# Writing ALiBi's distances with ScalarE into the scores' banks, the first projections by halves, and a new order of engine work

## The reference

```python
def _L0_attn_ref(hidden_states, Wq, bq, Wk, bk, Wv, bv, Wo, bo, alibi_slopes):
    ...
    scores = jnp.einsum('bhsd,bhtd->bhst', q, k)
    rel = (pos[None, :] - pos[:, None]).astype(scores.dtype)
    bias = alibi_slopes[:, None, None] * rel
    scores = (scores + bias[None]) / math.sqrt(HD)
    scores = 30.0 * jnp.tanh(scores / 30.0)
    scores = jnp.where(causal[None, None], scores, -jnp.inf)
    probs = jax.nn.softmax(scores, axis=-1)
    ...
x = x + _L0_attn_ref(_layernorm(x), ...)        # self attention, causal, ALiBi
x = x + _L0_xattn_ref(_layernorm(x), ctx_2048, mask_BxS2_bk0)   # one head, 128 memory tokens
x = x + _L0_ffn_ref(_layernorm(x), ...)         # silu(gate) * up, then down; weights rounded to fp8 e4m3
```

## Time and profile before

| | us |
|---|---|
| median of 3 runs (557.02 to 558.56) | 558.46 |
| the profiled execution | 558.21 |
| its span, first to last instruction | 556.4 |
| PE busy | 543.5 (98%) |
| DVE, POOL, ACT busy | 361.7, 287.1, 268.5 |
| DMA over the span | 50.74 MB, 91 GB/s |

### The profile page before, as it was taken

How to read it: one execution, slowest core, us unless ns; L and a number is a source line. 1 busy time by engine, 2 the same in 40 slices (tenths; PEclk the granted TensorE clock), 3 DMA queues, 4 the chain that set the end, 5 groups by cost and what they waited for, 6 DMA issues and landing times.

```text
span 556.4 us, 10168 instructions
## 1 busy us (share of the span) xinstructions
PE 543.5 (98%) x3962; PEld 427.4 (77%) x3962; DVE 361.7 (65%) x699; ACT 268.5 (48%) x485; POOL 287.1 (52%) x260
## 2 busy tenths in 40 slices
PE   7999999999999999999899999999999999999997
PEld 7788888888878888888687888766686667866675
DVE  7998877899596796659777886355623564244422
ACT  6848976777765785765743441033401333023310
POOL 5298898965774568787774346134400333013320
PEclk9999999999999999999899999999999999999999
DMA  8951231463217110148832712100011000100001
GB/s 306 347 199 39 78 99 54 124 194 103 77 39 223 43 58 21 58 153 258 275 150 77 264 26 89 57 1 0 1 38 39 0 1 0 58 19 1 0 20 57
DMA packets 43422, 50.74 MB, mean 91 GB/s; under 512 B 2544, under 2 KB 25072, under 8 KB 43376
## 3 DMA queue, kind: packets, MB, share of 16 engines
q1 hardware_dynamic: 43088, 49.58, 26.8%
q10 hardware_dynamic: 288, 0.52, 0.3%
HBM read 36.46 MB, written 13.63 MB: 90 GB/s over the span
## 4 chain that ended last, share of the span: by engine, by line
PE 83%; POOL 8%; DVE 4%; issue 2%; ACT 2%; DMA 1%; DVEq 0%; ACTq 0%; POOLq 0%
PE bank L287 34%; PE bank L452 23%; PE bank L472 16%; PE bank L282 2%; PE bank L394 2%; PE bank L379 2%; PE bank L404 2%; POOL q_w L740 2%; POOL q_w L738 2%; POOL probs L731 1%; POOL x_res L754 1%; PE bank L334 1%; DVE q_m L1228 1%; PE bank L371 1%; POOL reduced L723 1%
## 5 line engine op out<-in xcount | busy, mean ns | idle before, releaser
L287 PE MATMUL bank<-reduced 128*128 128x512 f32 x936 | 224.4, 396 | 1.5 <-ACT probs L897 1.1
L287 PEld LDWEIGHTS bank<-reduced 128*128 128x128 f32 x936 | 173.8, 189 | 39.8 <-issue 1.5
L837 POOL TENSOR_TENSOR f_parts<-fused,f_parts 128x512 fp32r<-128x512 f32 x48 | 62.5, 1301 | 159.9 <-ACT f_parts L1075 159.9
L1057 ACT ACTIVATE tanh_g<-bank,half_gate 128x512 f32<-128x512 f32 x48 | 33.0, 688 | 149.2 <-PE bank L452 139.0
L472 PE MATMUL bank<-reduced,f_parts 128*128 128x512 f32 x384 | 88.4, 390 | 0.0
L472 PEld LDWEIGHTS bank<-reduced,f_parts 128*128 128x128 f32 x384 | 71.9, 188 | 15.0
L1395 DVE SCALAR_TENSOR_TENSOR silu<-tanh_g,bank 128x512 f32<-128x512 f32 x48 | 32.9, 685 | 62.7 <-ACT tanh_g L1057 62.6
L452 PE MATMUL bank<-reduced 128*128 128x512 f32 x288 | 72.0, 402 | 0.0
L452 PEld LDWEIGHTS bank<-reduced 128*128 128x128 f32 x288 | 54.1, 188 | 12.9
L738 POOL TENSOR_TENSOR q_w<-q_w,q_m 128x512 f32<-128x512 f32 x36 | 49.6, 1379 | 9.2 <-DVE q_m L1230 9.2
L731 POOL TENSOR_SCALAR_AFFINE_SELECT probs<-probs 128x1024 f32<-128x1024 f32 x32 | 36.2, 1136 | 34.6 <-ACT probs L904 34.6
(11 more groups left out here) (119 smaller groups left out, 737.1 us busy)
## 6 DMA issues: line engine op xcount, KB each, us to landing
quantized<-q_w SPq DMA_DIRECT2D x36, 256.0 KB, 3.3
reduced<-quantized SPq DMA_DIRECT2D x12, 512.0 KB, 6.8
memT_sb<-in_memT SPq DMA_DIRECT2D x16, 256.0 KB, 5.1
mem_sb<-in_mem SPq DMA_DIRECT2D x16, 256.0 KB, 5.8
out<-y_sb SPq DMA_DIRECT2D x16, 256.0 KB, 2.0
q_w<-in_gate_w SPq DMA_DIRECT2D x12, 256.0 KB, 3.2
q_w<-in_up_w SPq DMA_DIRECT2D x12, 256.0 KB, 3.1
x_res<-in_x SPq DMA_DIRECT2D x3, 1024.0 KB, 9.4
```

Of the source, the lines that this page charges most:

```text
L287: ins = pe.matmul(dst, stationary, moving, start=(n == 0), stop=(n == len(pairs) - 1))
L837: pool.tensor_tensor(f_lo[:, f, :], fused[:, f % 2, :], f_hi[:, f, :].bitcast(F32), ALU.subtract).then_inc(f_lo_ready, 1)
```

## The change

Seven parts. (A) For (g, hg) = (1,1), (1,2), (2,2) and (3,2) the four matmuls of L371 are gone. ACT writes slope times distance into banks 2 to 5 instead, four instructions out of one 128x128 tile `distance`, made by POOL once all of `place_n` has been used. (B) The second halves of the first Q and K go to banks 6 and 7, each half is drained for itself, and the scores' third tile waits for them. (C) All four x tiles are loaded by SP; the high part of the first piece of Wq is made by POOL. (D) `bias_through` is put after the third V projection. (E) On POOL `low_part(g, 0)` stands between the two halves of `causal(g, 2)`, and `norm_scale(1, g-1)` behind both. (F) DVE: `cross(g-2, 6)` before the last slabs of hg 0; `masks` behind `norm_shift`; all four tiles of the second norm behind `x_low`. (G) At the feed forward's start `cross(2, 1)` on ACT and DVE is put ahead of two slabs, `high(0, 1)`, `fuse(0, 1)` and `normalize_context(3, 3)`, with the copy of T2 ahead of the exp; `gate_up` takes each bank only when its first matmul is due.

```diff
+SEEDED = ((1, 1), (1, 2), (2, 2), (3, 2))
...
+                first = [take((name, 0, 0), b) for name, b in (("Q", Q_BANK), ("K", K_BANK))]
+                second = [take((name, 0, 0), b) for name, b in (("Q2", C_BANK), ("K2", E_BANK))]
...
-                    pe.wait_ge(w_hi_made, m + 1)
-                    part(m, first, w_hi, xT_hi, start=True)
-                    if m == 0:
-                        turn_x(0, 3, S_BANK + 3)
+                pe.wait_ge(w_first_made, 1)
+                part(first, 0, w_hi, xT_hi, start=True)
+                turn_x(0, 3, S_BANK + 3)
+                pe.wait_ge(w_hi_made, 1)
+                part(first, 1, w_hi, xT_hi, start=True)
...
+                    if g == 0 and hg == 0 and i == 2:
+                        wait_drained(pe, ("Q2", g, hg))
+                        wait_drained(pe, ("K2", g, hg))
...
+            def scores_onto(g, hg):
+                dst = [take(("S", g, hg, j), S_BANK + j) for j in range(4)]
+                pe.wait_ge(seeded, (SEEDED.index((g, hg)) + 1) * 4)
+                wait_drained(pe, ("Q", g, hg))
+                wait_drained(pe, ("K", g, hg))
+                for i in range(GT):
...
+                        ins = pe.matmul(dst[j][0][:, t], kT[rows, t], qT[rows, t], start=False, stop=(i == GT - 1),
+                                        skip_group_check=True)
...
-                seats = [take((name, g, f), banks[w]) for w, name in ((0, "G"), (1, "U"))]
                 if g == 0:
-                    for w, (dst, done) in enumerate(seats):
+                    for w, name in ((0, "G"), (1, "U")):
+                        dst, done = take((name, g, f), banks[w])
...
-                    if g == 0 and i == 0:
+                    if g == 0 and i == 2:
                         bias_through()
...
-            for i in range(0, GT, 2):
+            for i in range(GT):
                 sp.dma_start(x_res[:, i, :], x_t[:, i, :]).then_inc(x_first_loaded[i], 16)
...
+                if i == 2:
+                    pool.wait_ge(raw_loaded[0], 16)
+                    pool.tensor_copy(w_hi[:, 0, :, FIRST], raw[0].rearrange("p (k n) -> p k n", k=KT)[:, :, FIRST])\
+                        .then_inc(w_first_made, 1)
...
+            pool.wait_ge(bias_made, 2 * HG)
+            pool.iota(distance[:], pattern=[[-1, S]], base=0, channel_multiplier=1,
...
+                slabs = slabs_at(ROUNDED, g, 2)
+                causal(g, 2, (0,))
                 if g:
                     low_part(g, 0)
+                causal(g, 2, (2,))
                 if g:
                     norm_scale(1, g - 1)
...
-                causal(g, 2)
                 low_part(g, 1)
...
+            def seed(g, hg):
+                if (g, hg) == SEEDED[0]:
+                    act.wait_ge(distance_made, 1)
+                for j in range(4):
+                    wait_drained(act, ("S", g, hg - 1, j))
+                    act.activation(bank[S_BANK + j][:].rearrange("p (i s) -> p i s", i=GT),
+                                   distance[:].unsqueeze(1).to_broadcast([P, GT, S]), ACT.Copy,
+                                   scale=slope_all[:, (hg - 1) * 4 + j:(hg - 1) * 4 + j + 1]).then_inc(seeded, 1)
...
-            for i in range(1, GT, 2):
-                act.dma_start(x_res[:, i, :], x_t[:, i, :]).then_inc(x_first_loaded[i], 16)
...
-            weight_high(0)
...
-            q_out(0, 0)
-            k_out(0, 0)
+            for items in (("Q", "K"), ("Q2", "K2")):
...
                     q_out(g, 1)
                     k_out(g, 1)
+                if g == 1:
+                    seed(g, 1)
...
                 q_out(g, 2)
                 k_out(g, 2)
+                if g:
+                    seed(g, 2)
...
             gate(0, 1)
+            cross(G - 2, 1)
             flag_slabs(slabs_at(FLAGGED, G - 1, 3))
             high(0, 1)
-            cross_first(G - 2, 1)
...
                     cross(g - 2, 5)
+                    cross(g - 2, 6)
                     prepare_slabs(slabs[2:])
-                    cross(g - 2, 6)
-                    masks(g - 1)
...
                     norm_shift(g + 1)
+                    if g >= 2:
+                        masks(g - 1)
...
-                if g:
-                    norm_apply(1, g - 1, g - 1, range(1))
...
-                    norm_apply(1, g - 1, g - 1, range(1, GT))
+                    norm_apply(1, g - 1, g - 1)
...
             fuse(0, 0)
+            cross(G - 2, 1)
             fuse(0, 1)
             normalize_context(G - 1, 3)
-            cross(G - 2, 1)
```

More of the change, by code:

```diff
@@ L327, in first_qk, with part @@
             def first_qk():
-                banks = [take((name, 0, 0), (Q_BANK, K_BANK)[m]) for m, name in enumerate("QK")]
-                def part(m, cols, w, t, start=False, stop=False):
-                    dst, done = banks[m]
+                first = [take((name, 0, 0), b) for name, b in (("Q", Q_BANK), ("K", K_BANK))]
+                second = [take((name, 0, 0), b) for name, b in (("Q2", C_BANK), ("K2", E_BANK))]
+                def part(half, m, w, t, start=False, stop=False):
+                    (dst, done), cols = half[m], slice(0, 2 * S) if half is first else slice(2 * S, TG)
                     for k in range(KT):
@@ L335, in part @@
                                         stop=stop and k == KT - 1)
-                    return ins, done
-                first, second = slice(0, 2 * S), slice(2 * S, TG)
+                    if stop:
+                        ins.then_inc(done, 1)
                 pe.wait_ge(xT_hi_ready, 2)
-                for m in range(2):
-                    pe.wait_ge(w_hi_made, m + 1)
-                    part(m, first, w_hi, xT_hi, start=True)
-                    if m == 0:
-                        turn_x(0, 3, S_BANK + 3)
+                pe.wait_ge(w_first_made, 1)
[3 more added lines that the diff above has]
+                part(first, 1, w_hi, xT_hi, start=True)
                 for i in range(2):
@@ L359, in first_qk @@
                 for m in range(2):
-                    ins, done = part(m, second, w_hi, xT_lo, stop=True)
-                    ins.then_inc(done, 1)
+                    part(second, m, w_hi, xT_lo, stop=True)
             def scores(g, hg):
@@ L445, in gate_up @@
                     return
+                seats = []
                 for n, high in enumerate((f % 2 == 0, f % 2 == 1)):
-                    for w, (dst, done) in enumerate(seats):
+                    for w, name in ((0, "G"), (1, "U")):
+                        if n == 0:
+                            seats.append(take((name, g, f), banks[w]))
+                        dst, done = seats[w]
                         for k in range(KT):
@@ L978, in _ @@
             act.wait_ge(small_loaded, 16)
-            q_out(0, 0)
-            k_out(0, 0)
+            for items in (("Q", "K"), ("Q2", "K2")):
+                for name, dst, bias in zip(items, (qT, kT), (bq_c, bk_c)):
+                    src, cols = wait_filled(act, (name, 0, 0)), slice(0, 2 * S) if name in "QK" else slice(2 * S, TG)
+                    act.activation(dst[:, cols], src[:, cols], ACT.Identity, bias=bias[:, 0:1])\
+                        .then_inc(drain_sem((name, 0, 0)), 1)
             weight_high(V_PART)
```

75 lines of the change are left out of this document (49 added, 26 removed).

## The result

The changed kernel takes 552.02 us (median of 6 runs, 551.94 to 552.46), the kernel before, run beside it, 557.75 (6 runs, 556.68 to 559.91). The ratio is 0.9888, 95% interval 0.9872 to 0.9904. The prediction was 551.4, in a range of 549.0 to 555.2. The profiled execution took 551.98, with a span of 550.0 against 556.4: 6.4 us less, where the sum had 7.03.

A forecast was written before the change was run, and what follows sets the result against it. PE, busy 98% of the span, was taken as the bound, with POOL second from 60 to 115 us. Terms of 0.77, 0.30, 0.75, 1.13, 0.34 and 3.74 made 7.03: 558.21 to 551.2, or 551.4 against the median; range 549.0 to 555.2.

The forecast's parts named there:

- Start (halves): At the first scores, K's products start at 16.64 rather than 17.41, as the first halves are long drained: 0.77 us gained.
- Start (x0 alone): At the kernel's start, the first x tile, issued first by SP, lands earlier: 0.3 us, between minus 0.2 and 0.87.
- x1 later than DVE wants it: Lower bound for loading x by SP alone: the second x tile comes too late for DVE, minus 0.2 us.
- POOL's order: At context(1,2), masks end at about 113.4 and bank 6 is late next: context starts 0.75 us earlier.
- POOL keeps the early gains: Rival, 60 to 115 us: slab loads set POOL's queue, so 1.07 and 0.75 are lost: 553.2 us; chance 0.13.
- Readout: At Q's projection, 156.44 us: DVE drains the last readout ahead of the slab, removing PE's whole 1.13 us wait.
- Seeds: Four score groups without bias matmuls: 0.34 us each for (2,2) and (3,2), nothing counted for (1,1) and (1,2).
- The ACT price: Four ACT writes into PSUM per seeded score group: 1.3 to 5.4 us, taken as 2.7.
- Feed forward's entry with seed (3,2): Exp placed first; gate_up(0,3) starts at 270.4 instead of 272.93 and runs at full clock: 3.74 us, 0.34 from the seed.
- The clock's 1.21: At gate_up(0,3), 28 products take 6.63 rather than 7.84 us because the clock does not fall: 1.21 us.
- The later feed forward "does not change": After the feed forward's entry: no wait there and no change, so nothing counted.
- the prediction's case of one more POOL instruction to wait out: At the feed forward's entry, norm tile 0 waits out another 1.3 us POOL instruction: gain there 2.4, time 552.5 us.

The follow-up runs named there:

- two queues again: The changed kernel with x's tiles 1 and 3 loaded by ACT again, tiles 0 and 2 by SP: 551.73 us, ratio 0.9879.
- the three other orders: The changed kernel with norm_scale and norm tile earlier near 303 us, low_part(1, 0) before both masks, gate_up(0,3)'s banks reversed: 551.49 us; repeated, 551.75 with seeds, 551.76 without.

## Why the prediction was right

The forecast was 0.6 us low, and its mechanism stands: five gains at five places, none taken back by a long wait. That the total came so close is in part luck. A lead counted 0.47 too high and a seed 0.2 too high stand against an entry 0.4 too low, and a gain of 0.6 that was not foreseen against a loss of 1.0. By its steps:

- **Start (halves): 0.77 predicted, 0.77 measured.** The copies took 0.47 where 0.48 was taken. Undone alone it costs 0.78 at the scores and 0.4 at the end.
- **Start (x0 alone): 0.30, measured 0.20, by luck.** The tile came 0.47 earlier as the argument has it, but then the third tile was late. The bound "x1 later than DVE wants it" was the right worry, about the wrong tile. The start moved from 0.17 later to 0.62 earlier than before over eleven traces, and with two queues again it was 0.29 earlier, so the 0.20 isn't shown to be the loads' doing.
- **POOL's order: 0.75 on top of a kept lead, to 1.82 at context(1,2); measured 1.35.** The next wait is the one named, bank 6 by DVE's L1236. Undoing the order costs 0.8 at the end, and the wait there grows by 0.94. What was too high is the lead brought there: bank 6 came free only 0.55 earlier (113.49 against 114.04), where the start's whole 1.07 was counted. Part of the start's gain is lost already at a mask (a wait of 0.32 us, at 54.6). That is what the rival "POOL keeps the early gains" had in mind, at a quarter of its size (0.47 of 1.82).
- **Readout: 1.13, measured 1.19,** and 1.2 of span when undone. That the row's releaser, tanh, was wrong is shown: with the old order in the new kernel, the profile itself names DVE.
- **Seeds: 0.34 each for two, measured 0.18 to 0.22.** This term was sized nearly twice too high. From the start of the four bias matmuls to PE's next work was 1.33 us at (1,2) (105.80 to 107.13); from the start of L406 it is 1.11 (104.86 to 105.97). The bias matmuls had covered the first weight loads of the scores (PEld's L379 began at 105.91, 0.23 ahead of its matmul), which now stand bare; that is the reading of these rows. The ACT price was right: 0.68 an instruction, 2.52 for four. At the end of the changed kernel no run shows a gain from seeds, as the two traces differ in the store; with the three other orders a gain of 0.6 is there at the end.
- **Feed forward's entry with seed (3,2): 3.74, measured 4.1** (3.9 of it where the lead goes from 3.0 to 6.9). The wait at bank 6 is 0.31 and not 0.95. The prediction charged 0.95 for the fourth norm tile, the mean of three unlike ones (0.95, 1.52 and 0.54); the tile that was added took 0.54. PE also came some 0.3 later than summed. The clock's 1.21 is in it, rightly for these two traces; over many executions it is a chance. The kernel before is clean in 3 of 31, the changed one in all six.
- **The later feed forward "does not change": wrong twice.** The lead grows by 0.6 between 274 and 298, where small waits are gone; that this is `gate_up` taking its banks one by one fits the places, but no run undid it. And the wait near 303 takes 1.0. PE comes there 7.5 us earlier, and now the weights' last store and the norm behind it are late; had the store been a short one, that loss would have been near zero, as in the trace without seeds. A chain that isn't set by PE must be timed against the lead that is forecast, not against PE before.

The Trainium skill (DMA: Bandwidth & Descriptors, "Issuing engines are not separate DMA queues") says that DMAs of all issuing engines interleave on the same 16 DMA engines, and that a second issuer saves only issue time. The traces agree in that the second issuer gained nothing. They add that the order of issue matters to a single tile: x0's reader started at 3.37 to 3.70 with x1 issued behind it (eleven traces), and at 4.02 to 4.42 with x1 beside it (three).

The other rule weighed, the exclusive lock (the Trainium skill, SBUF — State Buffer, "SBUF: two separate sides"), did strike norm tiles, but no more of them than before. One by one the four took 0.94, 1.52, 0.53 and 0.54 us. The first two each ended 0.29 behind a POOL instruction that had begun before them, and the other two began while POOL was idle. Before, the three took 0.95, 1.52 and 0.54, so the prediction's case of one more POOL instruction to wait out did not occur. The lock shows elsewhere too: a DVE product of 128x1 from two SBUF operands, 0.16 us elsewhere in the same loop, took 1.28 from 299.39 to 300.67, and POOL's L883 ended at 300.66. Four other traces have the same (0.36 to 1.14 us, each up to the end of POOL's instruction). Here DVE had time for it.

## What to carry to other kernels

Undo the parts one by one: the entry (2.7 us, and 1.6 more when the clock falls), the readout (1.2), POOL's order (0.8) and the halves (0.4 at the end, 0.8 at their place) make the result, and all of them only reorder work so that what PE waits for is done first. Replacing matmuls by another engine's writes gave less than the matmuls' own time, as they had hidden weight loads. Before two spans a few tenths apart are compared, line up their first matmuls, and take a mean over merged rows apart before it is used as a price. Before counting a lead to the end, look for the chains that PE doesn't set (a last store, a norm behind it on a slow engine): the lead runs into them.

## What the runs showed of the hardware

- The same idle stretch of PE seems to be followed by the 1.2 GHz level in some executions and not in others: with 2.65 us of waiting, 2 executions of 4 had the lower mean clock, and took 1.6 us longer. The one traced was at 1.00 behind the wait; the kernel before was at 0.50 behind its 2.27 us. With PE kept at work in the stretch, 15 of 16 executions of two kernels were clean. The Trainium skill (TensorE: Matmul & The Clock Gate, "What's actually happening") has the monitor running freely and not in step with the kernel; the scatter agrees with that.
- ACT writing 128x512 from SBUF into PSUM took 0.68 us with a scale for each partition, and a copy of that size from SBUF to SBUF 0.62 without one (L981). Out of PSUM ACT took 0.60 without such an operand (L920) and 0.67 with one, a bias (L929), so the operand can be the whole difference. The Trainium skill (ScalarE: Activation LUTs, "Step-by-step: what each stage is for") calls PSUM the faster target; no run here shows it either way.
- A 256 KB store took 2.15 to 2.24 us from its issue to the waiting copy in six traces, and 2.78 to 3.27 in the eight in which a 16 KB packet of the queue `q8 instruction` started 0.05 to 0.35 us after its issue; one kernel has a trace of each kind.
- A DVE instruction beside one of POOL's can stretch to that one's end: a norm tile of 0.54 us took 1.52, and a product of 128x1 of 0.16 us took 1.28.
